# Tensor product of a graph layer: spherical factors multiplied in after the turn to feature rows, one weighing and a quarter of the product on GpSimd

## The reference

```
def tensor_product(x_e, sh, w, C):      # x_e [E,64], sh [E,9], w [E,128], C [64,9,128]
    acc = sh[:, 0:1] * (x_e @ C[:, 0, :])
    for s in range(1, S):
        acc = acc + sh[:, s:s + 1] * (x_e @ C[:, s, :])
    return acc * w
k = tensor_product(x_dst, edge_sh, wk, Cqk).reshape(-1, H, DQK)
v = tensor_product(x_dst, edge_sh, wv, Cv).reshape(-1, H, DV)
attn = jnp.einsum('ehd,ehd->eh', q[edge_src], k)
amax = jax.ops.segment_max(attn, edge_src, num_segments=n)
ex = jnp.exp(attn - amax[edge_src])
```

## Time and profile before

| | |
|---|---|
| median of 3 runs | 3733.17 us (3731.1 to 3734.09) |
| the profiled execution | 3729.88 us, its span 3728.2 us, mean granted clock 0.942 |
| busy share of the span | PE 89%, PEld 85%, DVE 77%, ACT 34%, POOL 55% |
| layer 0 loop | about 35 to 1237 us |
| interlude | 1237 to 1414 us |
| layer 1 loop | 1414 to 3584 us |

### The profile page before, as it was taken

How to read it: one execution, slowest core, us unless ns; L and a number is a source line. 1 busy time by engine, 2 the same in 40 slices (tenths; PEclk the granted TensorE clock), 3 DMA queues, 4 the chain that set the end, 5 groups by cost and what they waited for, 6 DMA issues and landing times. The chain is left out here.

```text
span 3728.2 us, 86642 instructions
## 1 busy us (share of the span) xinstructions
PE 3330.0 (89%) x25947; PEld 3178.9 (85%) x25947; DVE 2877.5 (77%) x5292; ACT 1285.0 (34%) x3333; POOL 2055.4 (55%) x1999
## 2 busy tenths in 40 slices
PE   2099999999999337999999999999999999999963
PEld 1088888888888237999999999999999999999953
DVE  4366666666666227999999999999999999999943
ACT  1033333333333113444444444444444444444420
POOL 2577777777777435555555555555555555555540
PEclk9599999999999658999999999999999999999975
DMA  8399999999999313444444444444444444444420
GB/s 339 86 268 280 279 279 279 279 280 279 279 280 279 105 46 105 127 126 132 131 124 129 131 129 124 130 132 126 125 132 132 124 128 131 130 124 129 132 78 29
DMA packets 843789, 622.16 MB, mean 167 GB/s; under 512 B 490431, under 2 KB 732803, under 8 KB 843452
## 3 DMA queue, kind: packets, MB, share of 16 engines
q1 hardware_dynamic: 667110, 500.09, 44.2%
q0 software_dynamic: 56640, 87.65, 9.7%
q10 hardware_dynamic: 119982, 33.79, 4.1%
HBM read 335.87 MB, written 286.31 MB: 167 GB/s over the span
## 5 line engine op out<-in xcount | busy, mean ns | idle before, releaser
L1305 POOL DMA_INDIRECT xg<-h_tab,src_i x808 | 861.5, 1066 | 220.8 <-issue 127.2
L789 POOL DMA_INDIRECT kv<-kv_tab,src_i x808 | 762.1, 943 | 285.7 <-issue 188.2
L1315 POOL TENSOR_TENSOR kq<-kvs,q_of 128x512 f32<-128x512 f32 x202 | 260.6, 1290 | 837.7 <-DVE kvs L1491 837.7
L1401 ACT ACTIVATE z_hi<-bank 128x512 fp32r<-128x512 f32 x808 | 439.4, 595 | 802.9 <-PE bank L1333 802.9
L1357 PE MATMUL bank<-C_hi,z_hi 128*128 128x256 f32 x4040 | 682.2, 299 | 0.0
L1357 PE MATMUL bank<-C_lo,z_hi 128*128 128x256 f32 x4040 | 612.2, 281 | 0.0
L1481 DVE TENSOR_TENSOR z_lo<-bank,z_hi 128x512 fp32r<-128x512 f32 x808 | 520.5, 686 | 113.5 <-ACT z_hi L1401 113.4
L1357 PEld LDWEIGHTS bank<-C_hi,z_hi 128*128 128x128 f32 x4040 | 537.8, 191 | 0.3
L1357 PEld LDWEIGHTS bank<-C_lo,z_hi 128*128 128x128 f32 x4040 | 535.3, 188 | 0.0
L1357 PE MATMUL bank<-C_hi,z_lo 128*128 128x256 f32 x3232 | 516.2, 281 | 0.0
L913 DVE TENSOR_TENSOR wsb<-bank,b 128x512 f32<-128x512 f32 x404 | 279.3, 691 | 298.7 <-PE bank L977 298.3
(11 more groups left out here) (248 smaller groups left out, 4754.4 us busy)
## 6 DMA issues: line engine op xcount, KB each, us to landing
w_tab<-wsb SPq DMA_DIRECT2D x202, 512.0 KB, 3.4
win<-w_tab SPq DMA_DIRECT2D x202, 512.0 KB, 3.6
sum_edge<-rowt SPq DMA_DIRECT2D x202, 288.0 KB, 2.5
q_edge<-zq SPq DMA_DIRECT2D x202, 256.0 KB
qs<-q_edge SPq DMA_DIRECT2D x202, 256.0 KB, 2.8
sum_edge<-rows ACTq DMA_DIRECT2D x202, 136.0 KB
qs<-q_edge SPq DMA_DIRECT2D x202, 128.0 KB
drow<-dst_tab SPq DMA_DIRECT2D x202, 128.0 KB, 3.2
```

The costliest lines, as they stand in the source:

```text
L789: pool.indirect_dma_start(kv[b][:, q, :], None, kv0_tab, bass.IndirectOffsetOnAxis(ap=src_i[:, i * Q + q:i * Q + q + 1], axis=0))\
L1305: pool.indirect_dma_start(xg[b][:, q, :], None, h1_tab, bass.IndirectOffsetOnAxis(ap=src_i[:, i * Q + q:i * Q + q + 1], axis=0))\
L1315: pool.tensor_tensor(kq[:, :].rearrange("p (q o) -> p q o", q=Q), kvs[b][:, :, 0:O1], q_of[b % 2][:, :].rearrange("p (q o) -> p q o", q=Q) ...
L1401: nc.scalar.activation(z_hi[b % 2][:, k, :], bank[ZB[k]][:, :], ACT.Copy).then_inc(hi_out, 1)
```

## The change

z is no longer made with edges on partitions and turned. x alone is turned (`turn_x`: 2 transposes a step), ScalarE copies it from PSUM twice, so that both halves of the partitions hold the 64 features (`take_x`: four copies of 64x256), and z is made with features on partitions, in SBUF. For that, sh is needed with edges in the free dimension, the same row on 64 partitions: the interlude now loads sh, ScalarE reorders it and SP stores two tables (`sh_tab`, `sh_last_tab`), and each step loads 128 partitions x 8 KB of it, repeated (`load_sh`), and 128 x 1 KB for the last factor.

VectorE makes three of the four full blocks of z in one instruction (`outer`) and the last block in two (`outer_last`); GpSimd makes the fourth (`z_part`). `hi` and `lo` read z from SBUF in two pieces of 128x1024 and a last one. `weigh` moves from VectorE to GpSimd. x is gathered five steps ahead. The q rows get a PSUM bank of their own.

```diff
-                    unrolled([(times_q, -1), (gather_x, 4)], RING)
+                    def z_part(it, i, b):
+                        pool.wait_ge(x_out, i + 1)
+                        pool.wait_ge(sh_in[b % 2], 32 * (2 * it + b // 2 + 1))
+                        need(pool, lo_out, i * 3 - 4)
+                        pool.tensor_tensor(z[b % 2][:, ZD, :], xT[b % 2][:, :], sh[b % 2][:, ZD, :], ALU.mult)\
+                            .then_inc(z_part_ready, 1)
+                    def weigh(it, i, b):
+                        pool.wait_ge(exp_done, i + 1)
+                        pool.tensor_tensor(va[b % 2][:, :, 0:O1].rearrange("p q (h d) -> p q h d", d=DH),
+                                          kvs[b][:, :, O1:2 * O1].rearrange("p q (h d) -> p q h d", d=DH),
+                                          bcast(va[b % 2][:, :, O1:O1 + H1], 3, DH), ALU.mult).then_inc(va_ready, 1)
+                    unrolled([(times_q, -1), (weigh, -2), (z_part, 2), (gather_x, 5)], RING)
...
+                    def turn_x(it, i, b):
+                        pe.wait_ge(x_got[b], 16 * Q * (it + 1))
+                        need(pe, x_out, i - 1)
+                        for h in range(Q // 2):
+                            ins = nc.tensor.transpose(bank[b % 2][:, h * P:(h + 1) * P],
+                                                      xg[b][:, 2 * h:2 * h + 2, :].rearrange("p r d -> p (r d)"), ident[:, :])
+                        ins.then_inc(x_mm, 1)
...
-                    pipelined(pe, [(t_z(0), 1), (t_z(1), 1), (turn_max, -2), (sums, -3), (m_acc(0), 0), (t_z(2), 1),
-                                   (t_z(3), 1), (m_acc(1), 0), (t_z(4), 1), (spread_q, 0), (m_acc(2), 0),
-                                   (turn_logits, -1), (m_acc(3), 0)], RING)
+                    pipelined(pe, [(turn_x, 3), (turn_max, -2), (sums, -3), (m_acc(0), 0), (m_acc(1), 0), (turn_logits, -1),
+                                   (spread_q, 0), (m_acc(2), 0), (m_acc(3), 0)], RING)
...
-                    pipelined(act, [(hi(0), 1), (hi(1), 1), (copy_max, -2), (weights, -2), (take_sums, -3), (hi(2), 1),
-                                    (hi(3), 1), (hi(4), 1), (take_q, 0)], RING)
+                    pipelined(act, [(hi(0), 1), (take_x, 3), (copy_max, -2), (weights, -2), (take_sums, -3), (hi(1), 1),
+                                    (hi_last, 1), (take_q, 0)], RING)
...
+                    def outer(it, i, b):
+                        dve.tensor_tensor(z[b % 2][:, 0:ZD, :], bcast(xT[b % 2][:, :], 1, ZD), sh[b % 2][:, 0:ZD, :],
+                                          ALU.mult).then_inc(z_ready, 1)
...
+                            dve.tensor_tensor(z_lo[b % 2][:, c, :], z[b % 2][:, c, :], z_hi[b % 2][:, c, :].bitcast(F32),
                                               ALU.subtract).then_inc(lo_out, 1)
...
-                    pipelined(dve, [(product(1), -1), (lo(0), 1), (lo(1), 1), (subtract, -2), (outer(0), 2), (lo(2), 1),
-                                    (lo(3), 1), (logits, -1), (weigh, -2), (outer(1), 2), (lo(4), 1), (build, 1),
-                                    (segment_max, -1), (product(0), 0)], RING)
+                    pipelined(dve, [(product(1), -1), (subtract, -2), (outer, 2), (logits, -1), (lo(0), 1),
+                                    (lo(1), 1), (outer_last, 2), (build, 1), (lo_last, 1), (segment_max, -1),
+                                    (product(0), 0)], RING)
```

More of the change, by code:

```diff
@@ L1064, in gnn @@
             tab_q, q1_scat, qf_got, qf_put = sem("tab_q"), sem("q1_scat"), sem("qf_got"), sem("qf_put")
+            SG = NST // 2
+            sh_rows = [sb(f"sh_rows{g}", [SG, ST, S], F32, ph) for g in range(2)]
+            sh_parts = sb("sh_parts", [SG, S, ST], F32, ph)
+            sh_padded, sh_rows_in, sh_rows_turn, sh_parts_set, sh_put = (
+                sem("sh_padded"), sem("sh_rows_in"), sem("sh_rows_turn"), sem("sh_parts_set"), sem("sh_put"))
             groups4 = [(a, min(a + 4, NJ)) for a in range(0, NJ, 4)]
@@ L1163, in _ @@
                                  .then_inc(c_out, 1)
+                    act.wait_ge(sh_rows_in, 48)
+                    for g in range(2):
+                        if g:
+                            act.wait_ge(sh_put, 32)
+                        for r in range(2):
+                            nc.scalar.activation(sh_parts[:, 4 * r:4 * r + 4, :],
+                                                 sh_rows[g][:, :, r:S - 1:2].rearrange("p e c -> p c e"), ACT.Copy)
+                        nc.scalar.activation(sh_parts[:, S - 1, :], sh_rows[g][:, :, S - 1], ACT.Copy)\
+                                 .then_inc(sh_parts_set, 1)
                     for g, (a, b) in enumerate(groups4):
@@ L1212, in gnn @@
             RING = 4
-            sh = [sb(f"sh{b}", [P, Q, S], F32, ph) for b in range(RING)]
+            sh = [sb(f"sh{b}", [P, 4, ST], F32, ph) for b in range(2)]
+            sh_last = [sb(f"sh_last{b}", [P, ST // 2], F32, ph) for b in range(2)]
+            xT = [sb(f"xT{b}", [P, ST], F32, ph) for b in range(2)]
             xg = [sb(f"xg{b}", [P, Q, D], F32, ph) for b in range(RING)]
@@ L1224, in gnn @@
             rows = [sb(f"rowt{b}", [P, Q, F2], F32, ph) for b in range(RING)]
-            z = [sb(f"z{b}", [P, Q, (S - 1) * D], F32, ph) for b in range(2)]
-            z_last = [sb(f"z_last{b}", [P, Q * D], F32, ph) for b in range(2)]
+            z = [sb(f"z{b}", [P, 4, ST], F32, ph) for b in range(2)]
+            z_last = [sb(f"z_last{b}", [P, ST // 2], F32, ph) for b in range(2)]
             z_hi = [sb(f"z_hi{b}", [P, 5, Q * P], F32R, ph) for b in range(2)]
@@ L1365, in turn_logits @@
                         pe.wait_ge(attn_ready, i + 1)
[L1367 to L1371, removed]
+                        need(pe, max_copied, i)
                         nc.tensor.transpose(bank[SHARED][0:Q * H1, 0:P], attn[b % 2][:, :], ident[:, :]).then_inc(attn_mm, 1)
@@ L1409, in take_q, with hi_last @@
+                        return stage
+                    def hi_last(it, i, b):
+                        act.wait_ge(z_last_ready, i + 1)
+                        need(act, a_mm, i * 2 - 2)
+                        for f, e in zip(rows_of, edges_of):
+                            ins = nc.scalar.activation(z_hi[b % 2][f, 4, e], z_last[b % 2][f, :], ACT.Copy)
+                        ins.then_inc(hi_out, 1)
                     def take_q(it, i, b):
@@ L1481, in stage, with lo_last @@
-                            dve.tensor_tensor(z_lo[b % 2][:, k, :], bank[ZB[k]][:, :], z_hi[b % 2][:, k, :].bitcast(F32),
+                            c = slice(2 * k, 2 * k + 2)
+                            dve.tensor_tensor(z_lo[b % 2][:, c, :], z[b % 2][:, c, :], z_hi[b % 2][:, c, :].bitcast(F32),
                                               ALU.subtract).then_inc(lo_out, 1)
                         return stage
+                    def lo_last(it, i, b):
+                        dve.wait_ge(hi_out, i * 3 + 3)
+                        need(dve, a_mm, i * 2 - 2)
+                        for r in range(2):
+                            f, g, e = rows_of[r], rows_of[1 - r], edges_of[r]
+                            ins = dve.tensor_tensor(z_hi[b % 2][g, 4, e], z_last[b % 2][f, :],
+                                                    z_hi[b % 2][f, 4, e].bitcast(F32), ALU.subtract)
+                        ins.then_inc(lo_out, 1)
```

146 lines of the change are left out of this document (73 added, 73 removed).

## The result

The changed kernel takes 7142.98 us (median of 4 runs, 7140.75 to 7146.15), the kernel before 3733.63 us beside it: 1.913 times the time (95% interval 1.910 to 1.917). The forecast was 4060 us, in a range of 3600 to 4130. The sign was right, the size was not: of 3410 us that came in, the forecast had 330. Where a kernel's runs scatter, its ratio is over the runs within 1.5% of its fastest.

A forecast was written before the change was run, and what follows sets the result against it. The loop before was taken as TensorE-bound, VectorE close behind. A step of 12.3 against 10.67 us, times 201, gave +328; +6 for interlude and fill on 3730 gave 4064, called 4060 us (range 3600 to 4130).

The forecast's parts named there:

- The sign: Whole kernel: the change was expected to make it slower, chance 0.61, against 0.35 for faster and 0.04 for same.
- DMA: the step that failed: Layer 1 loop loads: 2.6 MB a step take 9.2 us, no obstacle to a step of 10 us or more.
- Rival 4: Layer 1 loop: the change's loads bind the step if engines move under 211 GB/s; little chance, within the remaining 0.09.
- The rate itself: Layer 1 loop loads: the DMA engines move 277 GB/s, taken from layer 0 at 0.98 busy.
- The interlude: Between the layers: loading, reordering and storing sh adds 3 us (0 to 12), loads at 277 GB/s.
- The lock, both ways: Layer 1 loop: VectorE instructions with two SBUF inputs and GpSimd instructions reading SBUF wait for each other; chance 0.52.
- the walk: One layer 1 step: VectorE's 9.21 us plus waits of 1.3, 0.7 and 1.2, less up to 0.1, gives 12.3.
- VectorE's terms: Layer 1 loop: VectorE's instructions sum to 9.21 us a step (8.95 to 9.35), including z at 1.76.
- ScalarE: Layer 1 loop: four small copies come in, at most 0.6 us each; below 7 us a step, hidden.
- the two transposes: Layer 1 loop, TensorE: 18 transposes a step become 2, 1.72 us less, leaving 8.95 us of its own work.
- GpSimd: Layer 1 loop: three products at 1.43 us each plus gathers at 5.17 make 9.46 us a step; kq takes 1.30.
- TensorE's clock: Layer 1 loop: a fall to half matters only if TensorE's path grows beyond its spare 3 us; left in the upper end.

The follow-up runs named there:

- x from PSUM: Changed kernel, both slow loads reshaped, z whole on VectorE reading doubled x from PSUM, gathers a step earlier, `weigh` on GpSimd: median 3738.93 us over 12 runs.
- the loads mended: Changed kernel with each repeated sh load cut in two (64 copies outermost) and interlude groups of 112 and 90 rows: 3948.01 us, 1.0578 of the kernel before.
- the kernel with `weigh` back: Changed kernel with reshaped loop and interlude loads, `weigh` returned to VectorE, GpSimd keeping the fourth block of z: 3896.17 us, 1.0439 of the kernel before.
- the last kernel: Kernel reading doubled x from PSUM, gathers earlier, `weigh` on GpSimd, now loading only one of four sh rows per half in the loop: 3543.72 us, one run.

## Why the prediction was wrong, point by point

**DMA: the step that failed.** "At the 277 GB/s that the engines moved at 0.98 busy in layer 0, 2.6 MB take 9.2 us: no obstacle to a step of 10 us or more", and "1 MB, loaded a whole step ahead, has time". The bytes were right. But the sum divides them by the rate of all 16 engines, and this load has two packets in flight, for which it takes over 20 us of a step of 26.97. The kernel with 64 copies outermost shows it from one side (3069 us back), the kernel before with the extra load from the other (2923 us in). The sign was no luck: without this failure the change still costs 5.8%. Rival 4 had the right condition, loads that move less than 211 GB/s, and "I give it little" since they moved 277 in layer 0: that row says nothing about a load of another shape.

**The rate itself** was also off: with up to 16 packets in flight, the engines move 226 GB/s at a share of 1.01 (extra load on the kernel before), 247 at 1.04 (x from PSUM). 2.6 MB at 226 to 247 are 10.5 to 11.5 us; counting what is really moved in a step, 10.29 us x 246 GB/s = 2.53 MB. It does not bind at a step of 12.3; it does at 10.2.

**The interlude** was put at +3 us (0 to 12) "at 277 GB/s". It was 133 us later (first load at 1540.78 instead of 1408), by the same failure: transfers of 101 rows that go one packet at a time. Mended it is 10 us, inside the bounds.

**The lock, both ways** ("Where it fails") was right, and the changed kernel shows both directions in two pairs of rows. As a size it was somewhat high: the walk had 1.3 us of waiting for attn and 1.9 for the two z_lo; measured with the loads mended are 1.21, and 2 x (1872 - 1212) ns = 1.3 us. So the step was 11.7 instead of 12.3. The whole price of the change without its two slow loads is 215 us, 1.0578 times, where the forecast had 334.

**VectorE's terms** held: z of 1536 elements 1.76, as worked out; by starts (in the kernel with `weigh` back) a z_lo from SBUF 1.14 for 1.18, the z_last pair 0.87 for 0.80, the z_hi pair 0.88 for 0.85; the sum of 9.21 is borne out within 0.1 by the last kernel's step of 9.63 us, which has 0.5 us more z. **ScalarE** and the two transposes were hidden, as said; ScalarE is busy 971 of 2000 us with the loop's loads mended. **GpSimd**: its own products run at 1.26 to 1.30 alone, as kq.

**TensorE's clock** was left "in the upper end". In the slow loop TensorE is busy 41% at a mean granted clock of 0.69 of its 2.4 GHz, between its two levels; with a quarter of the load it is busy 96% at 1.00. In the slow loop it cost nothing that can be seen, since TensorE's weight loads wait 3181.6 us for VectorE's attn over the run.

The range went wrong with the cause: its upper end, 4130, was built from the bounds of the lock alone. The 0.83 that the range held rested on a list of rivals in which every load was taken to move at the rate of layer 0.

## What to carry to other kernels

Before a load's bytes are divided by a rate, read its access pattern: what stands outermost, on both sides, decides how many of its packets are in flight: two for a broadcast written with 2 in front, one for a table of 101 rows, 16 to 18 at the most for 64 copies. A low mean DMA share beside an engine that waits for a DMA is the sign of it. And a product moved to GpSimd beside VectorE instructions with two SBUF inputs is paid for by waits on both; one of those inputs in PSUM took 1.2 us a step away, which no division of the products between the engines did.

## What the runs showed of the hardware that was not expected

- The repeated reads did not scale with the engines: a packet of 8 KB takes 0.32 to 0.33 us with 2 outermost and 0.56 to 0.63 with 64 outermost, so that engines with a share of about 1 move 226 to 247 GB/s instead of 278 in layer 0. The number in flight does not explain it: of the second form, the packets with fewer than 2.5 such packets in flight in the mean took 0.49 to 0.56 us too. With a quarter of the load, in packets of 2 KB with as many copies of a row, a packet took 0.109 us. Whether the common source row, the packet's size or where the packets are written does it was not tried.
- The lock goes to the engine that comes first, and 0.008 us ahead were enough for GpSimd; where it was ahead by 0.006 us or less, VectorE had the lock. In 202 pairs of the same two instructions one always ran at its own time (GpSimd's 1.26 us, VectorE's 1.76) and the other took longer by what it waited (VectorE's 2.81 to 2.87 us, GpSimd's up to 2.89).
- A kernel whose z waited for its loads by 0.58 us a step scattered over 300 us from run to run (3666 to 3966), while one bound by VectorE at nearly the same DMA share stayed within 9 us. The cause is open.
